# Decoder block: cross-attention scores of 64 stationary columns a tile, TensorE's loop cut elsewhere, chunks scaled a slot later

## The reference, cut to what matters

```
x = x + _L0_attn_ref(_layernorm(x), wq, wk, wv, wo)
x = x + _L0_xattn_ref(_layernorm(x), ctx_4096, mask, Wq, Wk, Wv, Wo, q_norm_w, k_norm_w)
x = x + _L0_ffn_ref(_layernorm(x), ...)

def _L0_xattn_ref(...):                 # H, KVH, HD = 32, 8, 128
    q = (hidden_states @ Wq.T).reshape(b, 64, H, HD).transpose(0, 2, 1, 3)
    k = (states @ Wk.T).reshape(b, 64, KVH, HD).transpose(0, 2, 1, 3)
    v = (states @ Wv.T).reshape(b, 64, KVH, HD).transpose(0, 2, 1, 3)
    q = _rmsnorm(q, q_norm_w)
    k = _rmsnorm(jnp.repeat(k, 4, axis=1), k_norm_w)
    scores = jnp.einsum('bhqd,bhkd->bhqk', q, k) * scale + mask     # 64 x 64 each
    probs = softmax(scores)
    out = jnp.einsum('bhqk,bhkd->bhqd', probs, repeat(v))
    return out.transpose(0, 2, 1, 3).reshape(b, 64, H * HD) @ Wo.T
```

## Time and profile before

| | |
|---|---|
| median of 3 runs | 1753.78 us (1748.47 to 1756.14) |
| profiled execution | 1748.64 us, its span 1746.9 us |
| mean granted clock of TensorE | 0.986 |
| busy: TensorE, its weight loads | 1669.0 us, 1370.1 us |
| busy: VectorE, ScalarE, GpSimd | 1065.2, 764.9, 654.9 us |

### The profile page before, as it was taken

How to read it: one execution, slowest core, us unless ns; L and a number is a source line. 1 busy time by engine, 2 the same in 40 slices (tenths; PEclk the granted TensorE clock), 3 DMA queues, 4 the chain that set the end, 5 groups by cost and what they waited for, 6 DMA issues and landing times.

```text
span 1746.9 us, 32770 instructions
## 1 busy us (share of the span) xinstructions
PE 1669.0 (96%) x12760; PEld 1370.1 (78%) x12760; DVE 1065.2 (61%) x1977; ACT 764.9 (44%) x1396; POOL 654.9 (37%) x511
## 2 busy tenths in 40 slices
PE   5899899999999999899988999999999999998898
PEld 5566788888888888678875567888888888886797
DVE  4488666565665665764545876565656565657543
ACT  2575535354444453421226744445353544443221
POOL 3596423233233232550116944243233332335400
PEclk9999999999999999899999999999999999998999
DMA  4110011021010120211111102011010210201000
GB/s 168 60 43 1 21 42 61 0 60 42 18 60 18 42 66 0 73 49 38 59 60 51 31 1 60 3 60 31 29 60 0 60 44 16 66 25 61 7 19 25
DMA packets 26099, 71.14 MB, mean 41 GB/s; under 512 B 3120, under 2 KB 3376, under 8 KB 26032
## 3 DMA queue, kind: packets, MB, share of 16 engines
q1 hardware_dynamic: 26032, 70.22, 12.9%
HBM read 66.01 MB, written 4.19 MB: 40 GB/s over the span
## 4 chain that ended last, share of the span: by engine, by line
PE 85%; DVE 8%; POOL 3%; ACT 2%; issue 2%; DMA 1%; POOLq 0%; SPq 0%; DVEq 0%; ACTq 0%
PE acc L407 14%; PE acc L408 13%; PE acc L409 13%; PE y L407 9%; PE y L409 9%; PE y L408 9%; PE quad L665 7%; PE quad L692 4%; PE y L676 2%; PE quad L588 2%; DVE w_lo L1181 1%; POOL prob L1660 1%; PE quad L448 1%; PE acc L425 1%; DVE xn_lo L1181 1%
## 5 line engine op out<-in xcount | busy, mean ns | idle before, releaser
L1651 POOL TENSOR_TENSOR qkrs<-qkve,mhalf 128x10 f32<-128x10 f32 x64 | 124.9, 1952 | 350.6 <-DVE qkve L1332 350.6
L1660 POOL TENSOR_TENSOR prob<-prob,pmax 128x512 f32<-128x512 f32 x128 | 133.9, 1046 | 288.1 <-DVE pmax L1240 287.7
L407 PE MATMUL acc<-w_hi,xn_hi 128*128 128x512 f32 (+1 forms) x576 | 229.0, 398 | 11.1 <-DVE xn_lo L1181 11.1
L407 PE MATMUL y<-w_hi 128*128 128x512 f32 x576 | 232.7, 404 | 1.9 <-issue 1.9
L1326 DVE TENSOR_REDUCE qkss<-kbd 128x4 f32<-128x512 f32 x128 | 87.8, 686 | 234.5 <-ACT kbd L879 234.5
L408 PE MATMUL y<-w_lo,w_hi 128*128 128x512 f32 x576 | 226.0, 392 | 0.0
L409 PE MATMUL y<-w_hi,w_lo 128*128 128x512 f32 x576 | 226.0, 392 | 0.0
L408 PE MATMUL acc<-w_lo,xn_hi 128*128 128x512 f32 (+1 forms) x576 | 222.4, 386 | 0.0
L409 PE MATMUL acc<-w_hi,xn_lo 128*128 128x512 f32 (+1 forms) x576 | 220.6, 383 | 0.0
L1647 POOL TENSOR_TENSOR w_lo<-stage,w_hi 128x1024 fp32r<-128x1024 f32 (+1 forms) x88 | 169.9, 1939 | 111.6 <-ACT w_hi L845 111.6
L1666 POOL TENSOR_TENSOR prob<-prob,prec 128x512 f32<-128x512 f32 x128 | 148.4, 1159 | 79.7 <-DVE prec L1248 79.7
(11 more groups left out here) (129 smaller groups left out, 3716.4 us busy)
## 6 DMA issues: line engine op xcount, KB each, us to landing
stage<-in_w_cross SPq DMA_DIRECT2D x64, 512.0 KB, 3.6
stage<-in_w_cross SPq DMA_DIRECT2D x32, 256.0 KB, 3.0
stage<-in_w_ffn SPq DMA_DIRECT2D x16, 512.0 KB, 3.4
x<-in_x SPq DMA_DIRECT2D x8, 512.0 KB, 3.7
stage<-in_w_self SPq DMA_DIRECT2D x8, 512.0 KB, 4.5
kt<-in_ctx SPq DMA_DIRECT2D x16, 256.0 KB, 2.9
out_x<-x SPq DMA_DIRECT2D x16, 256.0 KB, 2.0
stage<-in_w_self SPq DMA_DIRECT2D x4, 256.0 KB, 3.4
```

The costliest lines, as they stand in the source:

```text
L407: nc.tensor.matmul(target, l_hi, r_hi, start=first, stop=False)
L1651: return nc.gpsimd.tensor_tensor(target, source, mhalf[:, 0:width], ALU.pow)
L1660: nc.gpsimd.tensor_tensor(pr, pr, spread(pmax[:, buffer, :], 8, SEQ), ALU.subtract).then_inc(s_sub.sem, 1)
```

## The change

- `scores2`: the stationary tile of 128 columns is now two of 64 (one query head each, h = 0, 1), which write the upper and the lower 64 PSUM partitions: 64 matmuls in place of 32, with the same moving keys.
- TensorE's `slot` begins with the outputs and ends with the queries' projection. What stood ahead of the first loop's output projections has gone into the prelude, and out of the last turn.
- VectorE's `scale_chunk` runs behind the row maximum of the next slot, ahead of the transposes, and no longer between the two residual updates.
- In the prelude the first scores come ahead of the projection of chunk 2, with the order of ScalarE and VectorE to match.
- The last turn has a new order on TensorE, ScalarE, VectorE and GpSimd. Two waits for `pt_done` are added there; the buffers' waits of `scores2` and `transpose_probs2` get an argument, since the order differs by place. The list FFN, which numbers the feed-forward part's banks, follows.

```
             def slot(place, k):            # TensorE
-                scores2(place, k + 1)
-                transpose_probs2(place.at, k)
-                project_chunk_kv(place, k + 3)
-                values2(place, k, k + 2)
-                project_chunk_q(place, k + 3)
                 outputs(place, k, 0)
                 outputs(place, k, 1)
+                scores2(place, k + 2)
+                transpose_probs2(place.at, k + 1, 2 * k)
+                project_chunk_kv(place, k + 4)
+                values2(place, k + 1, k + 3)
+                project_chunk_q(place, k + 4)
...
                         for i in range(4):
                             rows = slice(32 * i, 32 * (i + 1))
                             first = 32 * (1 - i % 2)
-                            ins = nc.tensor.matmul(quad[:, i, t * SEQ:(t + 1) * SEQ],
-                                                   q2t[rows, t, j].rearrange("p h q -> p (h q)"),
-                                                   k2t[rows, t, j, first:first + SEQ], start=j == 0, stop=j == 3)
+                            for h in range(2):
+                                ins = nc.tensor.matmul(
+                                    quad[h * SEQ:(h + 1) * SEQ, i, t * SEQ:(t + 1) * SEQ],
+                                    q2t[rows, t, j, 2 * h:2 * h + 2, :].rearrange("p h q -> p (h q)"),
+                                    k2t[rows, t, j, first:first + SEQ], start=j == 0, stop=j == 3)
...
                 project_out(at, NT - 1, NT)          # TensorE, prelude
+                scores2(first, 0)
                 project_chunk_kv(first, 2)
-                scores2(first, 0)
                 project_chunk_q(first, 2)
                 second_norm(7)
+                scores2(first, 1)
+                transpose_probs2(first.at, 0, -2)
+                project_chunk_kv(first, 3)
+                values2(first, 0, 2)
+                project_chunk_q(first, 3)
...
                 masked_scores(at, k + 1)             # VectorE, slot
                 row_max(at, k + 1, (k + 1) % PRING)
+                scale_chunk(at, k + 2)
                 transposed(place, k + 2)
...
                 variance(at, k + 3)
                 update_x(at, 2 * k)
-                scale_chunk(at, k + 3)
                 update_x(at, 2 * k + 1)
...
-                scores2(turn, 1)                     # TensorE, last turn
-                transpose_probs2(turn.at, 0)
-                project_chunk_kv(turn, 3)
-                values2(turn, 0, 2)
-                project_chunk_q(turn, 3)
+                transpose_probs2(turn.at, 1, -2)
+                scores2(turn, 2)
+                pe.wait_ge(pt_done.sem, turn.at(pt_done, 2))
                 outputs(turn, 0, 0)
-                scores2(turn, 2)
-                transpose_probs2(turn.at, 1)
+                values2(turn, 1, 3)
                 outputs(turn, 0, 1)
-                values2(turn, 1, 3)
+                transpose_probs2(turn.at, 2, 0)
                 norm(0)
+                pe.wait_ge(pt_done.sem, turn.at(pt_done, 3))
                 outputs(turn, 1, 0)
...
```

More of the change, by code:

```diff
@@ L656, in scores2 @@
                 pe.wait_ge(s_add.sem, at(s_add, k))
-                pe.wait_ge(ot_lo_done.sem, at(ot_lo_done, max(k - 1, 0)))
+                pe.wait_ge(ot_lo_done.sem, at(ot_lo_done, max(k - 1, 0) if after is None else after))
                 for t in range(2):
@@ L774, in norm @@
                     layernorm_tile(at, A3[half][f"ln{i}"], 0, i)
-                scores2(turn, 1)
-                transpose_probs2(turn.at, 0)
-                project_chunk_kv(turn, 3)
-                values2(turn, 0, 2)
-                project_chunk_q(turn, 3)
+                transpose_probs2(turn.at, 1, -2)
+                scores2(turn, 2)
+                pe.wait_ge(pt_done.sem, turn.at(pt_done, 2))
                 outputs(turn, 0, 0)
-                scores2(turn, 2)
-                transpose_probs2(turn.at, 1)
+                values2(turn, 1, 3)
                 outputs(turn, 0, 1)
-                values2(turn, 1, 3)
+                transpose_probs2(turn.at, 2, 0)
                 norm(0)
+                pe.wait_ge(pt_done.sem, turn.at(pt_done, 3))
                 outputs(turn, 1, 0)
+                values2(turn, 2, 3)
+                norm(1)
                 outputs(turn, 1, 1)
[L789 to L792, removed]
+                latent(0)
+                scores2(turn, 3, after=3)
+                outputs(turn, 2, 0)
                 norm(2)
-                latent(0)
-                outputs(turn, 2, 0)
+                outputs(turn, 2, 1)
+                transpose_probs2(turn.at, 3, 4)
                 norm(3)
-                outputs(turn, 2, 1)
-                transpose_probs2(turn.at, 3)
                 up(0, 0)
@@ L1029, in self_attention @@
                 queries(first, 1, 0)
+                sibling_keys(first.at, 0)
                 queries(first, 1, 1)
-                sibling_keys(first.at, 0)
+                exps(first.at, 0, 0)
                 keys_and_values(first, 2)
@@ L1114, in last_turn_and_ffn @@
                 slot(turn, 0, next_group=False)
+                evacuate_probs2(turn.at, 1)
+                exps(turn.at, 2, 2)
                 split_piece(place, 0)
+                outputs_hi(turn.at, 1)
+                evacuate_probs2(turn.at, 2)
+                norm_hi(0)
                 split_piece(place, 1)
-                evacuate_probs2(turn.at, 1)
+                norm_hi(1)
+                sibling_keys(turn.at, 3)
+                outputs_hi(turn.at, 2)
                 split_piece(place, 2)
[L1119 to L1122, removed]
+                exps(turn.at, 3, 3)
+                norm_hi(2)
                 split_piece(place, 3)
[L1124 to L1128, removed]
+                evacuate_probs2(turn.at, 3)
+                norm_hi(3)
                 split_piece(place, 4)
-                norm_hi(3)
                 split_piece(place, 5)
-                evacuate_probs2(turn.at, 3)
                 rectify(0, 0)
@@ L1416, in self_attention @@
                 updated(7)
+                masked_scores(first.at, 0)
+                row_max(first.at, 0, 0)
                 scale_chunk(first.at, 1)
+                transposed(first, 1)
                 key_squares(first, 2)
-                masked_scores(first.at, 0)
-                transposed(first, 1)
-                row_max(first.at, 0, 0)
                 second_norm(7)
+                sums(first.at, 0, 0)
                 query_squares(first, 2, 0)
-                sums(first.at, 0, 0)
                 query_squares(first, 2, 1)
@@ L1533, in last_turn_and_ffn @@
                 row_max(turn.at, 1, 1)
+                scale_chunk(turn.at, 2)
                 transposed(turn, 2)
@@ L1540, in last_turn_and_ffn @@
                 variance(turn.at, 3)
-                updated(0)
-                scale_chunk(turn.at, 3)
-                final_statistics(0)
                 masked_scores(turn.at, 2)
                 row_max(turn.at, 2, 2)
-                transposed(turn, 3)
[L1547 to L1552, removed]
+                updated(0)
+                final_statistics(0)
+                sums(turn.at, 2, 2)
+                norm(0)
+                scale_chunk(turn.at, 3)
+                outputs_lo(turn.at, 1)
+                updated(1)
+                final_statistics(1)
+                norm(1)
+                transposed(turn, 3)
                 norm_lo(0)
+                norm_lo(1)
                 updated(2)
                 final_statistics(2)
-                updated(3)
+                outputs_lo(turn.at, 2)
+                latent(0)
                 norm(2)
@@ L1559, in last_turn_and_ffn @@
                 row_max(turn.at, 3, 3)
-                norm_lo(1)
+                updated(3)
                 final_statistics(3)
-                outputs_lo(turn.at, 2)
-                norm_lo(2)
-                latent(0)
                 sums(turn.at, 3, 3)
```

29 lines of the change are left out of this document (14 added, 15 removed).

## The result

| | before | changed |
|---|---|---|
| median of 7 runs | 1753.78 us (1748.47 to 1757.04) | 1743.33 us (1741.79 to 1745.38) |
| ratio to before | 1 | 0.9941, 95% interval 0.9925 to 0.9957 |
| span of the profiled execution | 1746.9 us | 1740.5 us |

The change gains 10 us where 48 were forecast; the time lies 3 us above the range. The forecast stood on a score block of 1.10 us and on rival E (instruction fetch) being unlikely. Both failed. The score block gave half of what was forecast, and rival E was the case.

A forecast was written before the change was run, and what follows sets the result against it. TensorE was taken as the bound: 85% of the chain, busy throughout the loop turns read. 1748.6 - 50.4 + 18 - 8 - 4 = 1704, given as 1706 us against a median; range 1678 to 1740 us.

The forecast's parts named there:

- rival E: TensorE's loops: the longer body no longer stays in the engine, instructions are fetched at jumps back; 0 to 30 us, chance 0.13.
- Scores, -50.4: TensorE's score blocks: 64-column tiles shorten each from 1.94 to 1.10 us, 0.84 in 60 of 64 blocks, -50.4 us.
- Starts 0.007 apart need 8 x 0.007 = 0.053: Score block: eight pair starts a round take 0.053 us, just below the 0.057 reload, so the reload sets the round.
- Rival D: Score block: pairs bound by issue, 0.027 us each, 128 in 3.4 us; decides from 0.014; 1842 us, chance 0.07.
- Rival C: Score block: two column halves of a row strip load in turn, round stays 0.111 us; 1745 us, chance 0.08.
- Collision, +18: First slot of each loop turn: VectorE's later scaling alternates with GpSimd's splits, TensorE waits 1.3 us, 14 times, +18 us.
- rival B: First slot of a turn: the collision costs nothing, the query scaling is not shut out or wins; 1688 us, chance 0.27.
- Prelude, -8: Ahead of each loop: masks before scaling remove TensorE's 2.94 us wait and half clock, 4 us a half, -8 us.
- Last turn, -4: Last turn of each half: about 6 us of waits again, less lost to the clock, 2 a half, -4 us.
- VectorE operations on SBUF alone stall beside GpSimd: VectorE's scaling beside GpSimd: such operations are held off, as when a pair took 2.73 us instead of 0.61.

The follow-up runs named there:

- e1: Changed kernel with 47 and 55 tiny matmuls added ahead of the two loops, so each TensorE loop body touches 7 instruction packets, not 8; 1734.43 us, 0.9901.
- e7: Changed kernel with 23 tiny matmuls ahead and none between the halves, so both loop bodies still touch 8 instruction packets; 1747.94 us, 0.9984.
- e4: Changed kernel with the padding of e1 and VectorE's scaling of chunks back between the two residual updates; 1727.64 us, 0.9864.
- e6: Changed kernel with the padding of e1, and weight piece 5 split by VectorE behind the scaling, not by GpSimd ahead of it; 1718.12 us, 0.9805.
- e8: Kernel before with the 64-column score tiles alone, plus 14 and 55 tiny matmuls so each loop body touches 7 packets; 1720.88 us, 0.9822.
- e2: Kernel before with the 64-column score tiles alone, without padding; TensorE's loop order, scaling and last turn as before; 1786.34 us, 1.0204.
- e5: Changed kernel with eight score blocks outside the loops in other forms, scores partly left out; 1759.91 us, which says nothing as a time.
- e10: e6, and in the last turn VectorE makes the low half of chunk 1's outputs ahead of scaling chunk 3; 1716.51 us, 0.9806.

## Why the prediction was wrong

- **Scores, -50.4: the step that failed first.** It is "Starts 0.007 apart need 8 x 0.007 = 0.053", carried from a burst of eight to 128 pairs. The reload was sized right (0.058 for 0.057). The first rounds of eight pairs run near it (32 pairs in 0.27); then the pairs themselves set the pace, 0.0115 us each, so a round takes 0.092, and the block is 1.53 us instead of 1.10. The term is -26.9. Rival D had the right mechanism, the pairs and not the load as the limit, with the wrong price: it took 0.027 from a stretch that the load had set. Its threshold was wrong too. The pairs decide from 0.057 / 8 = 0.007 us on; at 0.014 nothing is left of the gain. Rival C is out: by it a round takes 0.111, and the measured ones take 0.067 at first and 0.092 later.
- **Rival E, 0.13, was the case.** The price worked out for it, 1.2 us or more and 14 in all, was too low: a jump takes 4.9 us, of which the queue hides 3.9, TensorE starts again 0.56 behind its end, and 20.6 us are lost in the loops, 1.7 in each of 12 turns. Its argument was right in what it counted, the packets touched. What it lacked was where in a packet the body begins: 188 instructions ahead remove it (e1), 92 don't (e7).
- **Collision, +18.** The mechanism and the order of the engines came out as forecast (low half at 12.16 for 12.64), and rival B fell. Its price in a turn is 0.76 (e4), not 1.3: TensorE comes 0.42 later than forecast and the low half 0.48 earlier. In the changed kernel the wait is hidden under the jump, and it adds nothing to E there. That the loops lost 20.6 where the sum had 18 is luck: another cause took the place of this one, which without the jump costs 9 (e1: 4.5 in each loop).
- **Prelude, -8: nothing gained (+0.45).** The masks' wait went, and VectorE's low half came late in its place, 2.92 us, with the clock at 0.54 for the 3.5 us behind it. The collision had been worked out for the loops and not for the loop's entry, where GpSimd has the same two splits.
- **Last turn, -4: -1.3, within what can't be told.** The wait for the low half behind the scaling was forecast at 3 to 4 us and is 3.89.
- By the measured sizes the sum is -6.4 for the forecast -44.4. Of the 38 us between them the scores are 23.5, the prelude 8.5, the last turn 2.7, the loops 2.6 and the untouched stretches 0.7. With the scores alone put right the forecast would have been 1730, inside its range; the time left the range only with the prelude, the last turn and the loops on top.
- One statement of the prediction is too wide: "VectorE operations on SBUF alone stall beside GpSimd". In the kernel before, the transposes of the queries (L1234, from SBUF to SBUF) lay wholly beside GpSimd's work 78 times and took 0.67 us each time, as alone. It didn't change the sum, which held back only the scaling.

The Trainium skill, "Runtime: NRT & Kernel Launch", Instruction fetch mechanics, was cited for 128 KiB in blocks of 16 KiB. The packets are of 16 KB. By the Trainium skill's figure an estimated eight of them would fit. The runs show one less: bodies that touch 7 packets stay (e1, e6, e8), those that touch 8 are fetched at each jump (changed, e2, e7). The rule of the Trainium skill, "TensorE: Matmul & The Clock Gate", Back-to-back issue gap, some 25 ns between matmuls of few columns, doesn't hold for pairs on different tiles: 8.4 to 13 ns here on the mean, and 38 only where the pairs reload one tile in turn (e5: 4.77 us between first and last start of 128).

## What to carry to other kernels

Before you lengthen a loop on TensorE, count its instructions in packets of 256 and ask how many it touches from where it begins. A look at the sequencer's jump (0.2 us, or 3 to 5) tells it at once, and a few hundred idle instructions ahead can be worth more than the change: padding took 65 us off e2. A rate read from a burst of eight pairs did not hold beyond the 32nd, so price a long row of tiny matmuls by their count as well. When two engines shut each other out, work the collision out at every place where the moved instruction now stands, the entry and the last turn too.

## What the runs showed of the hardware that was not expected

- A jump back of 4.7 to 5.4 us (changed, e7) or 3.3 to 3.9 (e2) when the loop touches 8 packets, 0.21 when it touches 7 or fewer. All of the loop is fetched again, 9 packets a turn, and each of these jumps ends 2.3 to 2.8 us behind the start of a packet.
- Tiny matmul pairs on eight or more tiles start 0.0084 us apart or less for the first 32, then 0.0085 to 0.0133 apart, by their columns and keys and by the length of the row.
- Without a jump, a long row of such pairs outran the packets. In e5 TensorE stood 1.85 us in the middle of 256 pairs. In e8 it stood 1.11 behind 117 pairs of a plain block ahead of the loop, as its timeline shows:

```profile
202.59 0.36 PE L673 MATMUL quad<-kt,qb 32*64 32x64 f32 x11 [1.11 <-issue]
```

- A VectorE operation with a single large input (L1215, the normalisation, 0.50 us alone) was held off by a GpSimd split as well: 2.56 us (e10). It is so in the kernel before too, where ten of 32 are stretched, up to 2.6 us; the wait of 2.88 in the earlier trace rows ends with one of them, of 1.68. The transposes and the row maximum (0.69) never were.

Open: why the pace of the pairs changes behind the 32nd, and why a pair then takes 0.0115 us; and whether 7 packets are the most that stay for bodies of other lengths, since no run has a body between 1241 and 1753 instructions, or a longer one.
